# Gate rows of two experts side by side in one tile, their transfers issued after a weight piece's last split, and an expert down product that waits bank by bank

## What is computed

```python
probs = jax.nn.softmax(x @ router_w, axis=-1)
gates, idx = jax.lax.top_k(probs, 2)
gates = gates / jnp.sum(gates, axis=-1, keepdims=True)
dense_g = jnp.sum(jax.nn.one_hot(idx, n_exp, dtype=x.dtype) * gates[..., None], axis=-2)
g = jax.nn.silu(jnp.einsum('bsd,edh->bseh', x, w_gate))     # 8 experts, 192 -> 192
u = jnp.einsum('bsd,edh->bseh', x, w_up)
expert_out = jnp.einsum('bseh,ehd->bsed', g * u, w_down)
routed = jnp.einsum('bse,bsed->bsd', dense_g, expert_out)
shared = jax.nn.silu(x @ ws_gate) * (x @ ws_up) @ ws_down     # 192 -> 768 -> 192
alpha = jax.nn.sigmoid(x @ sg_w + sg_b)
return alpha * shared + (1.0 - alpha) * routed
```

## Time and profile before

| | us |
|---|---|
| median of three runs | 157.22 |
| lowest and highest of them | 156.07, 157.59 |
| the profiled execution | 155.41 |
| its span, first to last instruction | 153.5 |
| TensorE busy in the span | 134.4 (88%) |
| VectorE busy | 108.5 (71%) |
| ScalarE busy | 91.0 (59%) |
| GpSimd busy | 50.6 (33%) |

### The profile page before, as it was taken

How to read it: one execution, slowest core, us unless ns; L and a number is a source line. 1 busy time by engine, 2 the same in 40 slices (tenths; PEclk the granted TensorE clock), 3 DMA queues, 4 the chain that set the end, 5 groups by cost and what they waited for, 6 DMA issues and landing times.

```text
span 153.5 us, 4141 instructions
## 1 busy us (share of the span) xinstructions
PE 134.4 (88%) x1630; PEld 105.3 (69%) x1630; DVE 108.5 (71%) x280; ACT 91.0 (59%) x219; POOL 50.6 (33%) x63
## 2 busy tenths in 40 slices
PE   0239999999999989995679999998899999999991
PEld 0115887794478878984458868886587778787881
DVE  6389959989896999547475999857947623723753
ACT  0398695975997674683279868555544444444430
POOL 7000000500001432000005324586568386477430
PEclk9999999999999999999999999999999999999999
DMA  4999992780002323004995000485000000000003
GB/s 121 398 337 393 286 301 57 241 320 8 0 0 59 71 71 67 4 0 117 394 395 228 0 4 6 112 317 208 0 0 4 0 2 0 4 0 2 0 4 119
DMA packets 9941, 17.85 MB, mean 116 GB/s; under 512 B 2758, under 2 KB 6162, under 8 KB 9922
## 3 DMA queue, kind: packets, MB, share of 16 engines
q1 hardware_dynamic: 9562, 17.25, 34.0%
q10 hardware_dynamic: 360, 0.34, 0.8%
HBM read 16.63 MB, written 0.96 MB: 115 GB/s over the span
## 4 chain that ended last, share of the span: by engine, by line
PE 68%; DVE 10%; ACT 8%; issue 6%; ACTq 3%; POOL 2%; DVEq 0%; POOLq 0%
PE PS L684 20%; PE PS L714 10%; PE PS L458 4%; PE PS L408 3%; PE PS L495 3%; PE PS L573 3%; PE PS L542 3%; PE PS L431 2%; PE PS L429 2%; PE PS L432 2%; POOL vhl L1061 2%; DVE vhl L1448 2%; PE PS L556 2%; PE PS L395 2%; PE PS L599 2%
## 5 line engine op out<-in xcount | busy, mean ns | idle before, releaser
L1070 POOL TENSOR_TENSOR kq<-vhl,kq 128x296 f16<-128x296 f32 x35 | 28.7, 821 | 43.5 <-ACT kq L987 43.5
L1448 DVE SCALAR_TENSOR_TENSOR vhl<-PS,vhl 128x296 f32<-128x296 f32 x36 | 16.8, 465 | 19.9 <-POOL vhl L1061 10.5
L980 ACT ACTIVATE vhl<-PS 128x296 f32<-128x296 f32 x36 | 14.9, 415 | 24.3 <-PE PS L684 22.9
L987 ACT ACTIVATE kq<-vhl 128x296 f16<-128x296 f32 x36 | 16.0, 446 | 6.6 <-DVE vhl L1448 6.4
L1061 POOL TENSOR_TENSOR vhl<-vhl,xs 128x296 f32<-128x296 f32 x14 | 12.6, 899 | 5.6 <-issue 4.9
L1046 POOL TENSOR_TENSOR piece<-stage,piece 128x768 f16<-128x768 f32 (+1 forms) x3 | 4.6, 1525 | 22.7 <-DVE mx L1315 22.7
L1437 DVE TENSOR_TENSOR vhl<-vhl,xs 64x296 f32<-64x296 f32 (+1 forms) x18 | 10.2, 566 | 2.6 <-ACT vhl L980 2.4
L684 PE MATMUL PS<-XAh,piece 128*128 128x296 f16 x48 | 9.5, 290 | 1.6 <-ACT XAh L865 0.7
L684 PE MATMUL PS<-XAh,slab 128*128 128x296 f16 x48 | 10.0, 291 | 0.9 <-DVE vhl L1448 0.9
L431 PE MATMUL PS<-whl,xhl 128*128 128x193 f16 (+1 forms) x40 | 10.5, 263 | 0.0
L429 PE MATMUL PS<-whl,xhl 128*128 128x193 f16 (+1 forms) x40 | 10.5, 263 | 0.0
(11 more groups left out here) (233 smaller groups left out, 375.9 us busy)
## 6 DMA issues: line engine op xcount, KB each, us to landing
slab<-in_w_inner_dram SPq DMA_DIRECT2D x3, 960.0 KB, 9.5
xs<-gate_rows_dram SPq DMA_DIRECT2D x8, 296.0 KB, 5.7
xs<-in_x_inner_dram SPq DMA_DIRECT2D x3, 592.0 KB, 10.5
stage<-in_f_a_dram SPq DMA_DIRECT2D x2, 768.0 KB, 4.9
stage<-in_f_b_dram SPq DMA_DIRECT2D x2, 768.0 KB, 6.8
stage<-in_f_d_dram SPq DMA_DIRECT2D x2, 576.0 KB, 8.2
xhl<-in_f_a_dram SPq DMA_DIRECT2D x1, 768.0 KB, 9.3
xhl<-in_f_b_dram SPq DMA_DIRECT2D x1, 768.0 KB, 10.6
```

Source lines behind the costliest of these rows:

```text
L980: A(silu[:, i % 2, :], PS[:, 3 + 2 * (i % 2), 0:HALF], ACT.Silu, scale=1.0 / XW).then_inc(S["a_silu"], 1)
L987: A(ah[:, f % ABUF, half * HALF:(half + 1) * HALF], hf[:, i % 3, :], ACT.Copy).then_inc(S["a_ah"], 1)
L1070: G.tensor_tensor(al[:, f % ABUF, cols], hf[:, i % 3, :], ah[:, f % ABUF, cols], ALU.subtract).then_inc(S["g_al"], 1)
L1448: V.scalar_tensor_tensor(out=hf[:, i % 3, :], in0=PS[:, 4 + 2 * (i % 2), 0:HALF], scalar=SH / XW, in1=src[:, i % 2, :], op0=ALU.mult, op1= ...
```

## The change

Three edits:

1. `Gpair`, [128, 4, 592], is a view of the tile `stage`. For pair k of experts it holds the even expert's gate row on partitions 0 to 63 and the odd one's on 64 to 127. Two transfers of 64 partitions fill a pair, with one semaphore `d_gp[k]` for both. In a block of two experts `product(i)` multiplies with it in one instruction over 128 partitions; `Gb` is kept for the blocks of one expert.
2. As `stage` holds weight piece 1 until it is split, SyncE issues expert 0's row first, then waits for `a_fw` 12 and `v_fw` 9 (the end of both engines' splits of piece 1), and then issues pair 0, expert 1, expert 2, pair 1, expert 3, expert 4, pair 2, and so on to expert 7.
3. `down(6)` no longer waits for all five sums of VectorE before its first matmul, but for two before token tile 0, four before tile 2 and five before tile 4.

```diff
--- before.py
+++ after.py
@@ -200,6 +200,7 @@
             return up[:, 0], up[:, 1], up[:, 2], dn[:, 0], dn[:, 1]
 
         Gb = xs[:, 0:EXPERTS * N].rearrange("p (e n) -> p e n", e=EXPERTS)
+        Gpair = stage[:, 0:EXPERTS // 2 * N].rearrange("p (k n) -> p k n", k=EXPERTS // 2)
         g8 = whl[:, 0:480].rearrange("p (k t e) -> p k t e", k=12, t=TILES)
         lg = whl[:, 480:525].rearrange("p (t e) -> p t e", t=TILES)
         Gf = whl[:, 525:565].rearrange("p (t e) -> p t e", t=TILES)
@@ -219,6 +220,7 @@
         d_gb, d_cst, d_rows, d_tab, d_aw = sem("d_gb"), sem("d_cst"), sem("d_rows"), sem("d_tab"), sem("d_aw")
         d_f = [sem(f"d_f{i}") for i in range(PIECES)]
         d_g = [sem(f"d_g{e}") for e in range(EXPERTS)]
+        d_gp = [sem(f"d_gp{k}") for k in range(EXPERTS // 2)]
         d_gt, d_out = sem("d_gt"), sem("d_out")
         d_vw = [sem(f"d_vw{h}") for h in range(2)]
         d_vr = [sem(f"d_vr{h}") for h in range(2)]
@@ -365,8 +367,26 @@
             sp.wait_ge(S["a_gt"], 2)
             sp.dma_start(gate_rows[:, :], GT[:, 0:N]).then_inc(d_gt, 16)
             sp.wait_ge(d_gt, 16)
-            for e in range(EXPERTS):
+            def gate_of(e):
+
                 sp.dma_start(Gb[:, e, :], gate_rows[e:e + 1, :].to_broadcast([P, N])).then_inc(d_g[e], 16)
+
+            def gate_pair(k):
+
+                for m in (0, 1):
+                    e = 2 * k + m
+                    sp.dma_start(Gpair[64 * m:64 * m + 64, k, :],
+                                 gate_rows[e:e + 1, :].to_broadcast([64, N])).then_inc(d_gp[k], 16)
+
+            gate_of(0)
+            sp.wait_ge(S["a_fw"], 12)
+            sp.wait_ge(S["v_fw"], 9)
+            gate_pair(0)
+            gate_of(1)
+            for k in range(1, EXPERTS // 2):
+                gate_of(2 * k)
+                gate_pair(k)
+                gate_of(2 * k + 1)
             for t0, t1_ in ((0, 2), (2, 4)):
                 sp.wait_ge(S["v_fin"], t1_)
                 sp.dma_start(out[t0 * P:t1_ * P, :].rearrange("(t p) d -> p t d", p=P),
@@ -704,10 +724,10 @@
                     pe.wait_ge(S["v_al"], 1)
                 if f == 0:
                     pe.wait_ge(S["v_pad"], 2)
-                if f == ST:
-                    pe.wait_ge(S["v_acc"], TILES)
                 Dh, Dl = split(f // PT_)[3:]
                 for t in range(TILES):
+                    if f == ST and t % 2 == 0:
+                        pe.wait_ge(S["v_acc"], min(t + 2, TILES))
                     tok = slice(t * P, (t + 1) * P)
                     o = PS[:, t // 2, D * (t % 2):D * (t % 2) + D]
                     for k, (a, w) in enumerate(((ah, Dh), (al, Dh), (ah, Dl))):
@@ -1429,14 +1449,15 @@
                 src = silu
                 f, half = divmod(i, 2)
                 if two_experts(f) or f == FT - 1:
-                    dve.wait_ge(d_g[f_expert(f)[0]], 16)
-                    dve.wait_ge(d_g[f_expert(f)[1]], 16)
                     cols = slice(half * HALF, (half + 1) * HALF)
-                    e0, e1 = f_expert(f)
-                    for r0, r1, e in ((0, 64, e0), (64, P, e1)) if e0 != e1 else ((0, P, e0),):
-                        last = V.tensor_tensor(sgate[r0:r1, i % 2, :], silu[r0:r1, i % 2, :],
-                                               Gb[r0:r1, e, cols], ALU.mult)
-                    last.then_inc(S["v_sg"], 1)
+                    pair = f_expert(f)[0] // 2
+                    if two_experts(f):
+                        dve.wait_ge(d_gp[pair], 32)
+                        g = Gpair[:, pair, cols]
+                    else:
+                        dve.wait_ge(d_g[EXPERTS - 1], 16)
+                        g = Gb[:, EXPERTS - 1, cols]
+                    V.tensor_tensor(sgate[:, i % 2, :], silu[:, i % 2, :], g, ALU.mult).then_inc(S["v_sg"], 1)
                     dve.wait_ge(S["v_sg"], 2 * ((f - ST) // 3 + (f == FT - 1)) + half + 1)
                 elif f >= ST:
```

## The result

The changed kernel takes 155.01 us (median of 22 executions, 153.27 to 157.22) beside 155.34 us for the kernel before (22 executions, 154.58 to 157.59). The ratio is 0.9922, with a 95% interval of 0.9894 to 0.9950: 0.8% faster, clear of no change. The ratio compares only executions within 1.5% of each kernel's fastest (medians 154.05 us for the changed kernel, 155.28 before), which is why it says more than the 0.33 us between the two medians of all executions. The median before, 157.22 in the three runs known at the time of the prediction, came down to 155.34 with nineteen more.

A forecast was written before the change was run, and what follows sets the result against it. TensorE, busy 134.4 of 153.5 us, was taken as bounding, stopped by late VectorE products and sums. Terms 0.39 + 0.07 + 0.45 + 0.38 - 0.07 = 1.22 us took the median 157.22 to 156.0 us; range 157.3 to 154.8.

The forecast's parts named there:

- The verdict: Whole kernel's time: chance 0.59 of lying within 1%, 0.36 of faster by over 1%, 0.05 of slower by over 1%.
- Block 7: Two-expert block ahead of steps 16 and 17: one 128-row multiplication for two removes their stops, 0.39 and 0.07 us.
- The margin of 0.15 us before step 19: TensorE's step 19: product 17 ends about 0.15 us before the step wants it, so no stop.
- The sums: VectorE's five sums before down(6): shorter VectorE queue and wait by banks together remove a 0.45 us stop.
- Blocks 10 and 13: Two-expert blocks: stops before steps 22, 23, 28 and 29 all go, 0.07 + 0.07 and 0.16 + 0.08 = 0.38 us.
- The stop counted at nothing: Block 16: no stop from paired 64-row multiplications stands on the beat there, so nothing was credited.
- the rival of a larger gain: Stops ended by GpSimd's products, as before step 15, partly go too: gain 2.0 us, 155.2 us; chance 0.2.
- The 0.07 us that step 25 was to keep: Step 25 hangs on a GpSimd product chained to step 22, so it keeps 0.07 us of step 23's gain.
- The transfers: SyncE's later gate-row issues: pair 0 lands at 103.1, needed at 106.13, cover 3 us to minus 0.8; no cost unless late.
- the breakeven L = 107.8: Pair 0's landing time at which the gain is used up, 8.4 us after the second issue.
- The wait did move to GpSimd: Rival: step 19 or 25 stops for GpSimd's gate product (L1061); gain only 0.3 to 0.7 us, 156.7 us; chance 0.25.
- The late pair: Rival: pair 0 lands late and holds up VectorE before product 14; 1% slower at L = 109.4, 158.8 us; chance 0.05.

The follow-up runs named there:

- The two experiments: Changed kernel, down(6) waiting for all five sums before its first matmul: ratio 0.9882. Kernel before, with only the bank-by-bank wait of down(6) added: ratio 0.9989.
- the three kernels with the old pair products: The kernel before (155.34 us), and it with only the bank-by-bank wait of down(6) (156.31 us) or only three VectorE splits moved (154.85 us).
- all sums awaited: Changed kernel, but down(6) waits for all five sums before its first matmul, as before the change: 154.50 us, ratio 0.9882.
- a tile of its own: Changed kernel, pair tile laid over the attention weights' staging tile, SyncE's wait for the splits removed: 154.29 us, ratio 0.9852.
- that kernel: Changed kernel, but SyncE waits for VectorE's 12th split instead of the ninth before issuing pair 0: 158.53 us, ratio 1.0191.

## Why the prediction was right, and where it was wrong

The mechanism was right: each stop forecast to go went, and the steps on TensorE start where the sum put them. Three other steps failed: the base of the sum, the step from the gain to the verdict, and a stop that was counted at nothing.

**The size and its base.** Forecast 1.22 us, 0.8% less; measured 0.78% by the ratio, 1.54 us (1.0%, inside the ratio's interval) in the stretch. The time itself was forecast as 156.0 and is 155.01. The step that failed there is the base: "So I take 1.2 from the median 157.22". I had seen that the profiled execution (155.41) was quicker than all three runs, and held the three for the better base; with 22 executions the profiled one was the typical one. From 155.34 the same 1.2 us gives 154.1, near the 153.9 to 154.0 of the changed kernel's executions at full clock. Nor had the sum a term for the clock: 11 of the changed kernel's 22 executions ran at a lowered mean clock, 2.1 us longer by the median. So the median of all of them lies between the two levels' 153.9 and 156.0, only 0.33 us under the kernel before, where the sum had 1.22.

**The verdict.** "Within 1%" had 0.59 and "faster" 0.36. The point lies within 1%, but the interval is clear of no change. The step that failed is "A difference of 1% is about what a measurement of this kernel can tell from none", for which the prediction gives no working; with 22 executions of each the interval was 0.0056 wide, and a gain that I had worked out stop by stop deserved to be called faster.

**Block 7** (0.39 + 0.07): right. The disturbed 0.90 us stayed, and step 16 is on its beat. The margin of 0.15 us before step 19 is what the trace shows too: product 17 ends at 114.18, and step 19 starts at 114.33.

**The sums** (0.45): right in size and in mechanism. That the shorter VectorE queue brings them in "almost in time" was a shade too careful; they are in time with 0.16 us to spare. Priced together with the wait by banks, the term hid that the two edits cover for each other. The two experiments show it.

**Blocks 10 and 13** (0.38): right, all four stops are gone.

**The stop counted at nothing** (the 0.3 us between 1.22 and 1.54). "In block 16 no stop of this kind stands on the beat, and I credit nothing" is true of steps 34 and 35. But the step before them, 33, stopped for 0.23 us, and it is not in the prediction's list: it waits for product 31, whose gating GpSimd does, and such stops were left to the rival of a larger gain. It went with the change. In the kernel before, GpSimd's gate product, VectorE's product 31 behind it, and TensorE's steps 32 and 33:

```profile
139.36 0.80 POOL L1061 TENSOR_TENSOR vhl<-vhl,xs 128x296 f32<-128x296 f32 x1
...
140.61 0.47 DVE L1448 SCALAR_TENSOR_TENSOR vhl<-PS,vhl 128x296 f32<-128x296 f32 x1 [1.36 <-POOL vhl L1061]
...
139.64 0.41 PE L684 MATMUL PS<-XAh,xsq 128*128 128x296 f16 x2
...
141.13 0.42 PE L684 MATMUL PS<-XAh,xsq 128*128 128x296 f16 x2
```

Step 33 was due at 139.64 + 1.26 = 140.90. VectorE began product 31 0.44 us after GpSimd's gate product had ended, where 0.08 to 0.10 is usual in that trace. In the three kernels with the old pair products (280 VectorE instructions) that pause is there, in those with 272 it is not. Why it comes and goes was not tried, so the cause of this 0.23 us stays open. The 0.07 us that step 25 was to keep I find as 0.07 more before step 24, and the last hundredths are the rounding of a dozen starts.

**The transfers**: hidden. Between the second issue and the use lie 6.7 us, as reckoned, and the landing of 3.7 us taken for the head of the queue was 2.9 to 3.0, so the cover was 3.7 us instead of 3. What the prediction calls eleven issues are fifteen, eight of them of half height; in bytes they are the eleven full heights of its sum. I had called the breakeven L = 107.8 for a use at 106.13 and step 16 at L + 1.1; measured, step 16 comes 1.03 us after VectorE resumes.

**The rivals.** The wait did move to GpSimd (13.8 us of VectorE's waiting instead of 10.5), but it cost TensorE almost nothing: only steps 15, 21, 24 and 25 stop, all but step 24 (0.09 us now, 0.02 before) by what they did before. Of the larger gain only the 0.23 us of step 33 came by itself. I had written that its two largest stops "meet the weight splits, which are untouched"; moving those splits gave it, 1.05 us more. The late pair has the price given, up to the point where TensorE's pause costs the clock as well, which I had not priced.

## What to carry to other kernels

Write out the engine's beat, list each late start against it, and ask for each which instruction one or two steps back ended it: an edit is worth the stops that hang on what it shortens, here 1.5 us for 4.2 us less of VectorE's busy time. Compare two profiles over a stretch that begins and ends on the bounding engine inside the changed stage: it came out as 42.57 to 42.59 us in four profiles (the changed kernel twice, all sums awaited, a tile of its own), while spans and medians carried a swing of 2.1 us, larger than the change. Where two engines both have idle time left (here VectorE 29% and GpSimd 67% of the span) and slow each other, look whether a long instruction of the one can stand in its own idle time instead of beside the other's critical one.

## What the hardware showed

**VectorE and GpSimd hold each other up.** GpSimd's gate product takes 0.81 us, and 1.53 us when it meets a VectorE split of 1.05 us with two inputs from SBUF; VectorE's multiplication takes 0.47 us, and 0.90 when GpSimd's remainder of 1.03 us is running. The added time is a little less than what is left of the other's instruction, by the same 0.14 us in three cases of the changed kernel: 0.72 us added with 0.86 left (104.66), 0.51 with 0.65 (116.56), 0.43 with 0.57 (107.77). That is near what the Trainium skill says in "SBUF — State Buffer", section "SBUF: two separate sides": the shared pair of ports is locked for a whole instruction, and the loser waits. The trace agrees, and moving the splits shows the same from the other side.

**Half-height transfers** were not slow at the head of the queue: two of 64 partitions are in use 3.0 us after the second issue (3.6 after the first), and one of 128 at an empty queue landed after 3.0 to 3.7 us. Behind others the mixed queue moved less. The last two columns are the busy share of the DMA engines and GB/s, in the kernel before:

```profile
103.00:104.00 1.00, 1.00 (x12) 0.86 (x10) 0.88 (x1) 0.40 (x1) 1.00 (x2) 1.00 1.05 412
```

And of the changed kernel:

```profile
108.00:109.00 1.00, 1.00 (x14) 0.97 (x13) 0.96 (x2) 0.42 (x1) 0.35 (x1) 1.00 0.98 313
...
113.00:114.00 1.00, 1.00 (x11) 0.80 (x10) 0.29 (x1) 0.18 (x1) 1.00 (x2) 1.00 1.07 197
```

With transfers of full height only, the three stretches from 102 to 105 us moved 393 to 419 GB/s at a share of 0.99 to 1.08, though the first full one, 98 to 99 us, moved 192 at 0.96. With both kinds mixed, the seven from 108 to 115 us moved 197 to 313 at 0.98 to 1.07, and in the run with a tile of its own single ones reached 386. No run sends half-height transfers alone, so their own rate in a full queue is not shown. The Trainium skill's rule ("SBUF — State Buffer", section "Door 1: The DMA port swizzle") that 64 partitions reach half of the rate would fit the mixed queue and does not show in the first landing. Nobody waited for it here.

**The clock.** It fell to its lower level after TensorE had been idle for 2.9 us on end, and the mean clock was lowered in all four executions of that kernel. It fell in some executions and not in others after a stretch in which TensorE was busy for 0.56 or 0.57 of 1.5 us. The eleven executions of the changed kernel at a lowered mean clock have a median of 156.0 us, the eleven at full clock 153.9: 2.1 us, more than this change brought. "TensorE: Matmul & The Clock Gate" of the Trainium skill, section "What's actually happening", lets the clock follow how busy TensorE has been of late. The fall after 2.9 idle us agrees with that; why the same work lowered it in some executions and not in others no run here shows.
